# One transformer layer on one core: attention heads in row groups of 32 partitions, stacks written through DRAM, and twelve feed-forward units moved inside the attention

## What is computed

```python
scores = jnp.einsum('bhqd,bhkd->bhqk', Q, K) * scale
attn = jax.nn.softmax(scores, axis=-1)
attended = jnp.einsum('bhqk,bhkd->bhqd', attn, V)
...
x = _layernorm(x + attended @ Wo + bo)
shared_out = jax.nn.silu(xf @ sw1) * (xf @ sw3) @ sw2
s = jax.nn.sigmoid(xf @ router_w.T)          # top 2 of 8 experts, gates normalised
h = jax.nn.gelu(jnp.einsum('nd,edh->neh', xf, ew1), approximate=False)
y = jnp.einsum('neh,ehd->ned', h, ew2)
routed_out = jnp.einsum('ned,ne->nd', y, comb)
x = _layernorm(x + shared_out + routed_out)
```

## Time and profile before

| | |
|---|---|
| time, median of 3 runs | 256.45 us (256.32 to 257.67) |
| the profiled execution | 257.25 us, span 255.5 us |
| TensorE clock granted, mean | 0.951 of 2.4 GHz |
| PE busy | 224.7 us, 88% of the span |
| DVE busy | 169.7 us, 66% |
| ACT busy | 135.9 us, 53% |
| POOL busy | 92.4 us, 36% |
| HBM read, written | 11.22 MB, 1.11 MB |

### The profile page before, as it was taken

How to read it: one execution, slowest core, us unless ns; L and a number is a source line. 1 busy time by engine, 2 the same in 40 slices (tenths; PEclk the granted TensorE clock), 3 DMA queues, 4 the chain that set the end, 5 groups by cost and what they waited for, 6 DMA issues and landing times.

```text
span 255.5 us, 4348 instructions
## 1 busy us (share of the span) xinstructions
PE 224.7 (88%) x1514; PEld 152.6 (60%) x1514; DVE 169.7 (66%) x353; ACT 135.9 (53%) x261; POOL 92.4 (36%) x174
## 2 busy tenths in 40 slices
PE   1875972999999999997599999999899999999990
PEld 1533852776777677675367776657585565666640
DVE  8953892878978979798148984225755555565654
ACT  2351720676776667766136668885676333434230
POOL 8678381000100105321236886642723732020203
PEclk9997995899999999999759999999999999999996
DMA  6267774504719165285200000009760000350002
GB/s 186 58 93 94 87 71 97 52 9 71 66 41 85 16 88 45 44 83 157 86 0 0 8 0 9 1 4 398 303 290 0 0 1 0 126 249 14 28 17 66
DMA packets 12629, 19.42 MB, mean 76 GB/s; under 512 B 1296, under 2 KB 11728, under 8 KB 11952
## 3 DMA queue, kind: packets, MB, share of 16 engines
q1 hardware_dynamic: 12176, 18.49, 33.6%
q0 software_dynamic: 144, 0.39, 1.0%
q10 hardware_dynamic: 288, 0.27, 0.4%
HBM read 11.22 MB, written 1.11 MB: 48 GB/s over the span
## 4 chain that ended last, share of the span: by engine, by line
PE 78%; DMA 7%; DVE 7%; issue 3%; ACT 2%; POOL 1%; SPq 1%; POOLq 0%; DVEq 0%
PE ring L824 18%; PE pv_bank L838 14%; PE max_bank L810 12%; PE max_bank L948 11%; DMA qstack<-top_rows 5%; DVE kstack L632 3%; DMA kstack<-qk_parts 2%; PE ring L794 2%; PE ring L796 2%; PE ring L795 2%; PE max_bank L796 2%; PE max_bank L795 2%; PE max_bank L794 2%; PE misc_bank L877 1%; PE misc_bank L888 1%
## 5 line engine op out<-in xcount | busy, mean ns | idle before, releaser
L672 DVE TENSOR_REDUCE top<-max_bank 128x2 f32<-128x512 f32 x128 | 83.8, 684 | 33.5 <-PE max_bank L810 32.4
L571 ACT ACTIVATE probs_mem<-ring 128x512 f32<-128x512 f32 x128 | 73.8, 597 | 45.0 <-PE ring L824 43.7
L824 PE MATMUL ring<-qstack,kstack 128*128 128x256 f32 x256 | 62.7, 330 | 9.4 <-DMA qstack<-top_rows 9.4
L824 PEld LDWEIGHTS ring<-qstack,kstack 128*128 128x128 f32 x256 | 40.3, 198 | 37.6 <-ACT probs_mem L571 25.1
L810 PE MATMUL max_bank<-kstack,qstack 128*128 128x256 f32 x256 | 55.2, 305 | 3.7 <-DMA kstack<-qk_parts 3.2
L810 PEld LDWEIGHTS max_bank<-kstack,qstack 128*128 128x128 f32 x256 | 41.9, 203 | 8.0 <-DMA kstack<-qk_parts 4.0
L838 PE MATMUL pv_bank<-probs_mem,v 128*18 128x256 f32 x512 | 41.3, 397 | 0.0
L948 PE MATMUL max_bank<-probs_mem,wf 128*128 128x512 f32 x64 | 32.4, 593 | 0.6 <-DVE probs_mem L743 0.6
L609 ACT ACTIVATE probs_mem<-ring 128x512 f32<-128x512 f32 x21 | 12.4, 598 | 19.5 <-PE ring L796 19.3
L477 POOL TENSOR_SCALAR rstd<-mv 128x2 f32<-128x2 f32 x8 | 1.8, 226 | 50.8 <-DVE mv L709 50.7
L743 DVE TENSOR_TENSOR probs_mem<-probs_mem,kstack 128x512 f32<-128x512 f32 x16 | 11.2, 698 | 11.1 <-ACT probs_mem L609 11.1
(11 more groups left out here) (143 smaller groups left out, 340.5 us busy)
## 6 DMA issues: line engine op xcount, KB each, us to landing
kstack<-gate_scratch SPq DMA_DIRECT2D x2, 2048.0 KB, 9.2
qstack<-gate_scratch SPq DMA_DIRECT2D x2, 2048.0 KB, 7.8
kstack<-qk_parts SPq DMA_DIRECT2D x24, 64.0 KB
wf<-w_ffn_dram SPq DMA_DIRECT2D x1, 1408.0 KB, 6.0
qstack<-qk_parts SPq DMA_DIRECT2D x9, 128.0 KB
xs<-x_dram SPq DMA_DIRECT2D x4, 256.0 KB, 5.2
kstack<-wf_hi SPq DMA_DIRECT2D x12, 64.0 KB
qstack<-wf_hi SPq DMA_DIRECT2D x6, 128.0 KB
```

The costliest lines, as they stand in the source:

```text
L571: nc.scalar.activation(probs[:, k // 2 % 4, c % 2 * 512:(c % 2 + 1) * 512], ring[k % NRING][:, :], ACT.Exp, scale=SCALE).then_inc(probs_ma ...
L672: dve.tensor_reduce(top[:, half, h:h + 3:2], max_bank[n % NMAX][:, :].rearrange("p (h k) -> p h k", h=2), AX.X, ALU.max).then_inc(max_take ...
L824: ins = mm(ring[k % NRING][:, j * S:(j + 1) * S], kstack[:, s, ab, r, kt * P:(kt + 1) * P], qstack[:, s, r, :], start=True, stop=True)
```

## The change

- A head gets 32 partitions instead of 128: 24 rows of parts (`GR`) and, for the scores, two more for the maxima (`KROWS`). Four heads stand in the four groups of 32 partitions of one tile, and four tiles (`NT`) hold the 16 heads. A matmul of scores or maxima has 26 or 24 partitions of weights and data, still 128 by 256. `qstack` and `kstack` hold all 2048 tokens at once and are never cleared or used again.
- The order is a list of slots (`lay_out_slots`). A slot `s` makes two heads' scores (both banks of the ring) and two heads' maxima for a later `m`, eight matmuls in turns over the four row groups, then the products with V, then jobs. There are 64 slots `s` (`NHALF`); 14 slots before them and 8 between them have none. In a slot PE first waits for both exponentials of the slot before.
- x comes from the host a second time, transposed (`x_t`), so that PE's transposes at L779 go. Batch 0's stacks are projected straight into their place with weights laid out by the host (`first`, four tiles of two matmuls; ACT makes a high and a masked low part, DVE the difference). The others are projected for units of 256, 256, 512, 512 and 512 tokens (`UNITS`), stored to DRAM by four DMAs for the keys and four for the queries (`store`), and fetched by two (`fetch`) after the stores have landed. The units 3 and 4 are projected in slots s = 2 to 8 and 10 to 16.
- The shift takes four DMAs instead of two. `y` moves from DVE to POOL. The routing of the third and fourth group of tokens moves from POOL to DVE.
- Silu is made from Tanh by ACT and two operations of DVE; the hidden values of shared units are no longer split, and their `down` is one fp32 matmul (recorded as two) instead of three.
- Twelve of 40 feed-forward units stand among the slots `s`: ten of the first group of tokens (units 0 and 1 in slots 38 and 40, the eight experts in two clumps of four extra slots ahead of s = 46 and s = 52) and the two shared ones of the second (slots 56 and 58). The feed-forward weights are loaded at s = 0 and split on POOL from s = 10. 28 units remain for the end.

```diff
-NAB, NPAIR = 2, 8
+NT = 4
 HPS = 4
-SPB = H // HPS
-NSTEP = NB * SPB
-NRING = 2
+NHALF = NB * NT * QT
 NMAX = 3
-LEAD = 6
-NSLOT = 4
 NE = 8
...
+NU = NSH + NE
+NHB = 4
 VW = HD + 1
-ROW0 = HD * NAB
-ZERO_ROW = 96
+GR = 3 * HD
+KROWS = GR + 2
...
+    for n, job in ((0, ("first", 0)), (0, ("first", 1)), (2, ("k", 1)), (3, ("first", 2)), (3, ("q", 1)), (5, ("first", 3)),
+                   (6, ("k", 2)), (6, ("store", (1, 1))), (7, ("q", 2)), (7, ("store", (1, 0))), (8, ("fetch", 1)),
+                   (8, ("v", 0)), (9, ("v", 1)), (9, ("store", (2, 1))), (9, ("store", (2, 0))), (9, ("fetch", 2)),
+                   (9, ("bo", 0)), (10, ("shift", 0)), (11, ("add bo", 0)), (12, ("v", 2)), (13, ("add bo", 1))):
+        slots[n].jobs.append(job)
...
+    clumps = {46: [2, 3, 4, 5], 52: [6, 7, 8, 9]}
+    tail_units = [NU + n for n in range(2, NU)] + [u for g in (2, 3) for u in range(g * NU, (g + 1) * NU)]
+    at, m, done = {}, 12, 0
+    for s in range(NHALF):
+        for n, u in enumerate(clumps.get(s, ())):
+            slot = Slot(None, m if m < NHALF else None)
+            m += 1
+            if done < s:
+                slot.pv.append(done)
+                done += 1
+            slot.jobs.append(("unit", u))
+            if n >= 2:
+                slot.jobs.append(("down", u - 2))
+            slots.append(slot)
+        slot = at[s] = Slot(s, m if m < NHALF else None)
+        m += 1
+        while done < s - 1:
+            slot.pv.append(done)
+            done += 1
+        slots.append(slot)
+    for s in range(NHALF, NHALF + len(tail_units) + 22):
+        slot = at[s] = Slot()
...
+    for s, unit in ((2, 3), (10, 4)):
+        put(s, ("load xT", unit))
+        put(s + 1, ("k", unit))
+        put(s + 2, ("q", unit))
+        put(s + 3, ("v", unit))
+        put(s + 4, ("store", (unit, 1)))
+        put(s + 5, ("store", (unit, 0)), ("fetch", unit))
+        put(s + 6, ("add bo", unit - 1))
+    put(0, ("load w", 0))
...
+    for s, u in ((38, 0), (40, 1), (56, 10), (58, 11)):
+        put(s, ("unit", u))
...
-        qstack = sb("qstack", [P, NSLOT, NPAIR, S], F32R)
-        kstack = sb("kstack", [P, NSLOT, NAB, NPAIR, S], F32R)
+        qstack = sb("qstack", [P, NT, TOK], F32R)
+        kstack = sb("kstack", [P, NT, TOK], F32R)
...
+                    if kind == "store":
+                        u, i = n
+                        (t0, size), k = UNITS[u], staged.index(("qk"[i], u))
+                        for c, part in enumerate(COPIES[i]):
+                            if part is None:
+                                sp.wait_ge(ones_set, 1)
+                                src = ones[:, 0:size]
+                            else:
+                                src = parts[(u - 1) % 2][:, i, part, 0:size].bitcast(F32)
+                                if not part:
+                                    sp.wait_ge(qk_hi_made, k + 1)
+                                elif u == 1:
+                                    wait_taken(sp, ("qk"[i], u))
+                                else:
+                                    sp.wait_ge(qk_lo_made, k - 1)
+                            dst = stack_dram[i][:, c, :, :, t0:t0 + size].rearrange("j d t s -> j (d t) s")
+                            sp.dma_start(dst, src).then_inc(stack_stored[u][i], 16)
+                    if kind == "fetch":
+                        t0, size = UNITS[n]
+                        for i in (1, 0):
+                            sp.wait_ge(stack_stored[n][i], 16 * 4)
+                            src = stack_dram[i].rearrange("j c d t s -> (j c d) t s")[:, :, t0:t0 + size]
+                            sp.dma_start(stacks[i][:, :, t0:t0 + size].bitcast(F32), src).then_inc(stack_loaded[n], 16)
                     if kind == "shift":
-                        wait_taken(sp, (kind, b))
-                        for ab in range(NAB):
-                            move(qstack[32 * ab:32 * ab + 2, b % NSLOT, :, :],
-                                 top_rows[16 * ab:16 * ab + 16, b % 2, :]).then_inc(shift_loaded[b % 2], 16)
-                        if b == 0:
-                            stack(3)
+                        wait_taken(sp, (kind, n))
+                        for j in range(HPS):
+                            sp.dma_start(qstack[32 * j + GR:32 * j + KROWS, :, n * S:(n + 1) * S].bitcast(F32),
+                                         top_rows[8 * j:8 * j + 8, n % 2, :].bitcast(F32)).then_inc(shift_loaded[n % 2], 16)
...
+                    if kind == "y":
...
+                        chain(pool.tensor_tensor(rstd1[:, :], rstd1[:, :], minus_half[:, 0:QT], ALU.pow))
+                        for t in range(QT):
+                            ins = pool.tensor_scalar(xs[:, QT * n + t, :], res1[:, t, :], mv1[:, t, 0:1],
+                                                     rstd1[:, t:t + 1], ALU.subtract, ALU.mult)
+                        ins.then_inc(y_made, 1)
...
+            for slot in slots:
+                s = slot.s
+                if s is not None:
+                    i = s // 2
+                    if i >= 2:
+                        act.wait_ge(pv_made, 2 * (i - 1))
+                    for r in range(2):
+                        act.wait_ge(scores_made, 2 * s + r + 1)
+                        nc.scalar.activation(probs[:, i % 2, s_heads(s)[r], :], ring_of(("scores", 2 * s + r))[:, :],
                                              ACT.Exp, scale=SCALE).then_inc(probs_made, 1)
...
+                            nc.scalar.activation(first_hi[:, i, :], bank[:, i * S:(i + 1) * S], ACT.Identity,
+                                                 bias=b1[:, i * NT + b:i * NT + b + 1]).then_inc(first_hi_made, 1)
+                        act.wait_ge(first_hi_made, 2 * b + 2)
+                        if b >= 2:
+                            act.wait_ge(first_done, 2 * (b - 1))
+                        for i in range(2):
+                            nc.scalar.activation(first_lo[:, b % 2, i, :], first_hi[:, i, :].bitcast(F32), ACT.Identity,
+                                                 scale=lo_rows[:, i:i + 1]).then_inc(first_lo_made, 1)
...
-            def clear(tile, n, cleared):
-                dve.tensor_copy(tile, zero_col[:, :].to_broadcast([P, n])).then_inc(cleared, 1)
-            for s in range(2):
-                clear(kstack[:, s, :, :, :].rearrange("p a r q -> p (a r q)"), NAB * NPAIR * S, k_cleared[s])
-                clear(qstack[:, s, :, :].rearrange("p r q -> p (r q)"), NPAIR * S, q_cleared[s])
...
+                            dve.scalar_tensor_tensor(out=act_out[:, b % 2, :], in0=act_out[:, b % 2, :], scalar=1.0,
+                                                     in1=ring_of((kind, b))[:, :], op0=ALU.add, op1=ALU.mult).then_inc(sh_read, 1)
+                            dve.wait_ge(sh_read, NSH * g + n + 1)
+                            dve.scalar_tensor_tensor(out=hid[:, b % NHB, :], in0=act_out[:, b % 2, :], scalar=0.5,
+                                                     in1=misc_of(("third", b))[:, :], op0=ALU.mult, op1=ALU.mult).then_inc(hid_made, 1)
...
-                if k >= NRING:
-                    pe.wait_ge(probs_made, k - NRING + 1)
-                for j in range(2):
-                    ab, r = heads[2 * (c % 2) + j]
-                    ins = mm(ring[k % NRING][:, j * S:(j + 1) * S], kstack[:, s, ab, r, kt * P:(kt + 1) * P],
-                             qstack[:, s, r, :], start=True, stop=True)
...
+            def scores(s, r, kt):
+                (b, t), j = divmod(s // 2, NT), s_heads(s)[r]
+                rows, k = slice(32 * j, 32 * j + KROWS), b * S + kt * P
+                ins = mm(ring_of(("scores", 2 * s + r))[:, kt * S:(kt + 1) * S], kstack[rows, t, k:k + P],
+                         qstack[rows, t, b * S:(b + 1) * S], start=True, stop=True)
...
+            def maxima(m, r, qt):
+                (b, t), j = divmod(m // 2, NT), m_heads(m)[r]
+                rows, q = slice(32 * j, 32 * j + GR), b * S + qt * P
+                ins = mm(max_bank[(2 * m + r) % NMAX][:, qt * S:(qt + 1) * S], qstack[rows, t, q:q + P],
+                         kstack[rows, t, b * S:(b + 1) * S], start=True, stop=True)
...
+                for t in range(QT):
+                    for r in range(2):
+                        if s is not None:
+                            scores(s, r, t)
+                        if m is not None:
+                            maxima(m, r, t)
+                for p in slot.pv:
...
-                            for j in range(NSH):
-                                pe.wait_ge(lo_made[j], g + 1)
-                                c = slice(W2 + j * P, W2 + (j + 1) * P)
-                                three(acc, wf_hi[:, c], wf_lo[:, c], sh_hi[:, j, tokens(g)], sh_lo[:, j, tokens(g)],
-                                      j == 0, False)
```

(51 more changed lines are left out.)

896 lines of the change are left out of this document (431 added, 465 removed).

## The result

The changed kernel takes 341.4 us (median of 4 runs, 338.5 to 345.2) against 256.4 for the kernel before on the same chip: 1.329 times as long, interval 1.313 to 1.345. The forecast was 244.5. The profiled execution of after has 341.6 us of span, 86 more than before.

What follows compares the result with a forecast made beforehand. PE was taken to bound the kernel, with 78% of the span hanging on it. 39 start + 143 attention + 54 end + 7.5 gave 243.5 of span, 245.25 with 1.75 around it, 0.8 less for the median: 244.5; range 232 to 264.

Steps and rivals of the forecast that it cites:

- The start: Time until the first scores run, forecast at 39 us against 42.99 in the kernel before.
- with 1 and 2 KB rows I take 300: Start: stores and fetches through DRAM move at 300 GB/s, so 1 MB and 2 MB take 10.5 us.
- 44 at 243: Start: first scores at 44 us if the DRAM transfers run at 243 GB/s.
- The rival of the slow detour: Stores and fetches through DRAM at 112 GB/s at full share: scores start at 68, 274 us in all; chance 0.08.
- staging units 3 and 4: Attention: four projections give ACT 2 x 0.69 each against its slack of 0.61, costing 3 us.
- fetch 2 and the shift issued by 35: Start: SP issues unit 2's eight stores (5.3 us), waits for them, then issues these transfers by 35 us.
- The slot: Attention: 1.80 us for each of 48 slots with maxima, 1.70 for the 16 without, 113.6 in all.
- A slot's other matmuls fit the rest: Attention: with PE's scores, maxima and V at some 0.3 + 0.55 us, its remaining work fits within the slot.
- The clock: Grouped matmuls leave PE at 1.2 GHz: slot 2.15, units some 10 us more, 276 us in all; chance 0.07.
- The units inside: Attention: twelve feed-forward units cost 23.4 us there, about what they would cost at the end, no gain of their own.
- The DVE rival: Attention: DVE's in-order waits make slots 2.0 us while there are maxima, +9.6, 254 us in all; chance 0.13.
- The end: After the attention: 28 units 46.2, last V products 1.1, PE's last jobs 4.9, DVE stalls 1.8: 54 us.

Runs made afterwards that it cites:

- the shape mended: The changed kernel with every store cut by group of 32 partitions, so the slowest dimension is 32 and not 4: 303.4 us.
- 280.9 (clock): The changed kernel without its stores into DRAM, plus one full-row fp32 matmul in each slot behind the first exponential: 280.9 us.
- 266.9 (units out): The changed kernel without its stores, with one full-row matmul per slot and all 40 units behind the attention: 266.9 us.
- the kernel with everything mended and computed: The changed kernel with stores by group, SP's order mended, y on DVE, one full-row matmul per slot, all units behind the attention: 268.0 us.

## Why the forecast was wrong, step by step

**The start (39; was 63.2).** The step that failed is "with 1 and 2 KB rows I take 300". The rate was taken from the length of rows alone; the shape of the store let a quarter of the engines work, at 101 GB/s. With the shape mended the rate was 221 and the start 44.4, near the sum's own "44 at 243", in part by luck: SP's issuing was another size than in the sum. The rival of the slow detour had the start nearest (68 for 63) from 112 GB/s at full share; it left out that the stores come twice more, inside the attention. So did the forecast, whose 3 us for staging units 3 and 4 gave their stores no price: PE waited 19.1 us for x behind them. The term "fetch 2 and the shift issued by 35" had SP's wait for the landing in it, but sized by the 300 and by 5.3 us for issuing eight stores; issuing took 15.75, and the last landed at 55.40.

**The slot (1.80 and 1.70).** Side by side was right, in matmuls and weight loads, and the loop of 1.70 to 1.75 was seen at full clock. "A slot's other matmuls fit the rest" was wrong: transposes, projections and `wo` stand behind V's 0.56 in the 1.09 of the exponentials and don't fit; at half clock V alone is 1.06, where the earlier trace rows have 0.63, and a plain slot lasts 1.98 (scores at 65.15, 67.13 and 69.11 in after).

**The clock (chance 0.07).** The mechanism was the rival's, and the reason for setting it aside, "slots keep it busy for half of their time", failed: time busy isn't what kept the clock up in these runs. 32 rows with no gap ran at 0.50 for 250 us; the start that was cited as evidence had full-row matmuls. The row cited for the fall was misread too: from 40 to 44 the clock is at half from the beginning and PE's 1.01 us lie at the end, from 42.99; what came before is a PE that stood still from 38.07. The rival's price, 32 us, can't be read from one pair: 9 to 12 and 16.7 us came back by one full-row matmul per slot, which costs PE time itself and doesn't cover the units.

**The units inside (23.4; 35).** The step that failed is "about what they would cost at the end". The 23.4 had 2.35 for each shared unit and 14 for the clumps; inside they cost 35, and 39 with the clock up, against 28 at the end. Out of the attention they brought 8 to 10 us and, with the clock up, 14 to 16.

**DVE and POOL.** The DVE rival (254) had its mechanism: DVE is last at places of the mended slots; PE waits 5.9 us for its maxima in the 131. That `y` would be free on POOL was wrong at least once: it is on the chain with 1.6 us at 74.04, and PE waits for it there.

**The end (54; 63.5).** PE works 57.7 of it, 5.5 more than forecast (why stays open; the clock there is 0.95), and stands 5.8, of which the forecast had 1.8. The longest wait, 3.2, is for the routing on DVE. The last 7.5 was right (7.6).

The chain of medians is 341.4 (after), 292.9 (no stores), 280.9 (clock), 266.9 (units out), against the 244.5 forecast; the kernel with everything mended and computed has 268.0. So of the 97 us missed, the stores with what SP's order puts behind them carry 48, the clock 12, the units 14, and some 22 lie in slots, `y` and the end. Without the upper runs (then 340.4, 289.5, 280.9, 264.5) it is 51, 9, 16 and 20. The split also hangs on the order in which the causes are taken away.

**Two sums of the prediction.** "7 in 213 us of everything from 43 to the end" should be 8: 143 + 54 + 7.5 is 204.5, against 212.5. And slots of 1.72 with a start at 35 give 237 by its own terms, not 232. Neither would have moved the range as far as 341.

## What to carry to other kernels

Matmuls packed into row groups issue side by side, but PE's clock can fall under them and take the gain back; look at the granted clock and at the durations in a stretch, and if a full-row matmul has to be added, put it where PE waits anyway. For a new transfer, estimate the share of the DMA engines from its shape before the rate from its row length, and write down what SP stands behind: a wait for a landing holds every later issue. A large load just ahead of a small urgent transfer is worth moving behind it only where its own consumer has time (6 to 7 us gained in one place, no gain seen in the other).

## What the runs showed of the hardware

The clock: 1.2 GHz for 250 us with PE busy without a gap while scores and maxima read 32 rows (clock 0.50, PE 20.00 of 20 us), and 2.4 GHz again once the full-row matmuls of the feed-forward followed each other. The Trainium skill ("TensorE: Matmul & The Clock Gate", "What's actually happening") lets the gate go by how busy PE has been; if that is read as PE's busy time in a profile, these rows differ from it, and they decide.

The profile's granted clock isn't the whole of it. In after the records give 1.00 all through the wait of 24.6 us and on to 84, but up to 73 the same matmuls last longer than at 165:

```profile
67.13 0.55 PE L841 MATMUL ring<-qstack,kstack 26*128 26x256 f32 x1 [1.19 <-ACT probs_mem L575]
...
67.86 1.06 PE L867 MATMUL pv_bank<-probs_mem,v 128*18 128x256 f32 x8
```

```profile
64.00:68.00 4.00, 1.67 (x20) 1.21 (x24) 2.61 (x5) 2.20 (x5) 0.00 (x0) 1.00 0.23 91
```

0.55 and 1.06 here, 0.35 and 0.63 there (1.06 is also what V takes where the records give 0.50): so in such a stretch the durations tell, and the mean clock of 0.76 over after's attention is, by these rows, too high.
